# Split expert weights in device memory: one row of 24 KB per partition, or blocks of 128 rows of 4 KB

## What is computed

```python
mod = (silu(c) @ wmod).reshape(8, 6, 1, -1)
sa, ca, ga, sb, cb, gb = mod[:, 0], ..., mod[:, 5]
h = layernorm(x) * (1 + ca) + sa
x = x + ga * attn(h, ...)          # projections k, v, r; a decayed running sum of k*v; output projection
h = layernorm(x) * (1 + cb) + sb
x = x + gb * ffn(h, ...)

def moe_group(x2, router_w, wg, wu, wd, top_k):       # 32 experts, top_k = 2
    expert_weights, expert_indices = top_k(softmax(x2 @ router_w))
    # tokens sorted by expert, xs = x2[tok]
    gate, up = ragged_dot(xs, wg), ragged_dot(xs, wu)  # 512 -> 256
    ys = ragged_dot(silu(gate) * up, wd)               # 256 -> 512
    return zeros_like(x2).at[tok].add(ys * weight)

ffn = (moe_group(group 0) * 2 + moe_group(group 1) * 2) / 4
```

## Time and profile before

| | |
|---|---|
| median of 3 runs | 4911.22 us (4901.27 to 4916.95) |
| profiled execution, its own time | 4905.73 us |
| its span, first to last instruction | 4904.0 us |
| granted TensorE clock, mean | 0.971 |
| TensorE busy | 4580.8 us, 93% |
| DMA packets, bytes | 434624, 1152.46 MB, 235 GB/s |
| first stage, about | 0 to 1935 us |
| tile stage, about | 1935 to 4904 us |

### The profile page before, as it was taken

One profiled execution on the slowest core, in us unless ns is written; L12 is line 12 of the kernel. 1 busy time (PEld: TensorE's weight loads), 2 busy tenths in 40 slices (PEclk: granted clock), 3 DMA queues, 4 the chain that ended last, 5 costly groups with the idle time before them and its releaser, 6 DMA issues.

```text
span 4904.0 us, 89177 instructions
## 1 busy us (share of the span) xinstructions
PE 4580.8 (93%) x22649; PEld 3764.6 (77%) x22649; DVE 3080.2 (63%) x6077; ACT 1651.2 (34%) x4093; POOL 2858.1 (58%) x2300
## 2 busy tenths in 40 slices
PE   6999999999999995889999998999999999999998
PEld 4877777777777774667777777888788888888887
DVE  5999999999999996444444444444344444444443
ACT  2444444444444442222222222332222222222222
POOL 2577777777777776445444454555455555555554
PEclk8999999999999997899999999999999999999999
DMA  6767666666666674889899989998998988988887
GB/s 240 234 200 228 195 222 196 214 200 220 207 200 227 196 226 159 261 271 285 252 279 280 280 238 270 294 278 223 290 239 222 260 221 242 258 231 221 220 222 195
DMA packets 434624, 1152.46 MB, mean 235 GB/s; under 512 B 59361, under 2 KB 59362, under 8 KB 415666
## 3 DMA queue, kind: packets, MB, share of 16 engines
q0 software_dynamic: 182512, 454.27, 39.3%
q1 hardware_dynamic: 231106, 619.79, 36.6%
q10 hardware_dynamic: 20736, 75.51, 4.2%
HBM read 719.35 MB, written 463.57 MB: 241 GB/s over the span
## 4 chain that ended last, share of the span: by engine, by line
PE 42%; DMA 12%; issue 4%; POOL 2%; DVE 1%; POOLq 0%; SPq 0%; ACT 0%; DVEq 0%
PE ps L1316 12%; PE ps L1318 12%; PE ps L1317 12%; DMA out<-c_yo,c_idx 11%; PE ps L1325 4%; PE ps L1344 2%; POOL out L1307 1%; POOL c_xg L1274 1%; DMA c_wt<-wsp_d 0%; POOLq L1299 0%; DVE c_yo L1571 0%; POOL list_d L1279 0%; DMA list_d<-pairs,sidx 0%; DMA c_lists<-list_d,c_rowu 0%; DVE c_xl L1559 0%
## 5 line engine op out<-in xcount | busy, mean ns | idle before, releaser
L1307 POOL DMA_INDIRECT out<-c_yo,c_idx x576 | 915.1, 1589 | 933.9 <-DMA out<-c_yo,c_idx 512.5
L1316 PE MATMUL ps<-c_wt,c_xh 128*128 128x512 f32 x2304 | 964.1, 418 | 24.9 <-issue 16.8
L1318 PE MATMUL ps<-c_wt,c_xl 128*128 128x512 f32 x2304 | 910.3, 395 | 0.0
L1317 PE MATMUL ps<-c_wt,c_xh 128*128 128x512 f32 x2304 | 904.0, 392 | 0.0
L1274 POOL DMA_INDIRECT c_xg<-h2g_d,c_idx x576 | 565.0, 981 | 507.6 <-DVE c_yo L1571 400.5
L1555 DVE TENSOR_TENSOR c_hh<-ps,c_sil 128x256 f32<-128x256 f32 x576 | 244.2, 424 | 913.5 <-ACT c_sil L1398 843.5
L1571 DVE SCALAR_TENSOR_TENSOR c_yo<-ps,c_wc,c_xg 128x512 f32<-128x512 f32 x576 | 432.3, 750 | 529.2 <-PE ps L1318 261.5
L442 PE MATMUL ps<-xTh,wTh 128*128 128x512 f32 x1536 | 625.9, 407 | 53.5 <-DVE xTl L818 46.9
L1403 ACT CAST c_xh<-ps 128x512 fp32r<-128x512 f32 x576 | 339.2, 589 | 962.2 <-PE ps L1325 874.2
L709 POOL DMA_INDIRECT list_d<-pairs,sidx x496 | 545.5, 1100 | 188.5 <-issue 123.9
L1398 ACT ACTIVATE c_sil<-ps 128x256 f32<-128x256 f32 x576 | 221.3, 384 | 1177.1 <-PE ps L1318 1105.3
(11 more groups left out here) (199 smaller groups left out, 7776.2 us busy)
## 6 DMA issues: line engine op xcount, KB each, us to landing
c_wt<-wsp_d SPq DMA_DIRECT2D x69, 2048.0 KB
sraw<-wex SPq DMA_DIRECT2D x290, 256.0 KB
wsp_d<-shigh SPq DMA_DIRECT2D x288, 256.0 KB
wsp_d<-sraw SPq DMA_DIRECT2D x288, 256.0 KB
c_wt<-wsp_d SPq DMA_DIRECT2D x69, 1024.0 KB
xin<-x SPq DMA_DIRECT2D x34, 1024.0 KB
h2g_d<-mod_d SPq DMA_DIRECT2D x128, 256.0 KB
out<-xin SPq DMA_DIRECT2D x32, 1024.0 KB
```

The costliest lines, as they stand in the source:

```text
L1307: nc.gpsimd.indirect_dma_start(out=out, out_offset=bass.IndirectOffsetOnAxis(ap=idx[:, n:n + 1], axis=0), in_=yo[:, n % 4, :], in_offset=N ...
L1316: nc.tensor.matmul(o, lh, rh, start=first, stop=False)
L1317: nc.tensor.matmul(o, lh, rl, start=False, stop=False)
L1318: return nc.tensor.matmul(o, ll, rh, start=False, stop=last)
```

## The change

`wsp_d` gets another shape. Before it had 64 x 128 rows (expert, partition) of 6144 floats. Now it has for each expert 6 blocks (`NW`) of 128 rows of 1024 floats (`WCOL`): block k holds columns 1024 k to 1024 k + 1023 of what was the row. In memory, the rows of the 128 partitions of one block lie one behind the other, 4 KB each, and the next block of the same partition is 512 KB further on. The stores of SP and ACT write the same pieces to their new places. The load takes 4 blocks (gate and up) or 2 (down), so that each partition gets 4 or 2 rows of 4 KB in place of one of 16 or 8 KB. Nothing else changes: not the number of DMAs, nor their bytes, waits and order.

```diff
+WCOL = 1024
...
+    NW = 2 * WROW // WCOL
...
-    wsp_d = nc.dram_tensor("wsp_d", (GE * P, 2 * WROW), F32, kind="Internal").ap()
+    wsp_d = nc.dram_tensor("wsp_d", (GE * NW * P, WCOL), F32, kind="Internal").ap()
...
-                    return wex[0], bass.ds(b * (4 * P) + e * P, P), bass.ds(b * (4 * P) + e * P, P), part
-                return wex[1], bass.ds(b * (2 * P) + (e - 4) * P, P), bass.ds(b * (2 * P) + (E + e - 4) * P, P), part
+                    return wex[0], bass.ds(b * (4 * P) + e * P, P), b * 4 + e, part
+                return wex[1], bass.ds(b * (2 * P) + (e - 4) * P, P), b * 2 + (E + e - 4), part
...
-                    _, _, rows, part = split_at(b, j)
+                    _, _, ex, part = split_at(b, j)
                     for col, tile in zip(PARTS[part], (shigh[:, j % 2].bitcast(F32), sraw[:, j % 4])):
-                        sp.dma_start(wsp_d[rows, col:col + C], tile).then_inc(stg_out[j % 2], 16)
+                        rows = bass.ds(ex * (NW * P) + col // WCOL * P, P)
+                        sp.dma_start(wsp_d[rows, col % WCOL:col % WCOL + C], tile).then_inc(stg_out[j % 2], 16)
...
+            def load(u, e, a, z, sem_):
+                rows = bass.ds(e * (NW * P) + a // WCOL * P, (z - a) // WCOL * P)
+                sp.dma_start(wt[:, u, a:z].bitcast(F32).rearrange("p (n c) -> p n c", c=WCOL),
+                             wsp_d[rows, :].rearrange("(n p) c -> p n c", p=P)).then_inc(sem_, 16)
...
-                        sp.dma_start(wt[:, u, a:z].bitcast(F32), wsp_d[bass.ds(e * P, P), a:z]).then_inc(sem_, 16)
+                        load(u, e, a, z, sem_)
...
-                for col, tile in zip(((0, 2048), (1024, 3072), (4096, 5120))[k], (sgh[:, k].bitcast(F32), stg[:, k])):
-                    act.dma_start(wsp_d[rows, col:col + 1024], tile).then_inc(stg_out[k], 16)
+                for part, tile in zip(((0, 2), (1, 3), (4, 5))[k], (sgh[:, k].bitcast(F32), stg[:, k])):
+                    rows = bass.ds(x * (NW * P) + ((E + EA) * NW + part) * P, P)
+                    act.dma_start(wsp_d[rows, :], tile).then_inc(stg_out[k], 16)
```

More of the change, by code:

```diff
@@ L169, in stage_a @@
     xf, mod_d, h2g_d, list_d, wsp_d = L["xf"], L["mod_d"], L["h2g_d"], L["list_d"], L["wsp_d"]
-    ROWS = L["ROWS"]
+    ROWS, NW = L["ROWS"], L["NW"]
     R = TJ * G
@@ L1150, in stage_c @@
     GU = 2 * KC * 2 * H
+    NW = L["NW"]
     W = 4
@@ L1423, in split_out @@
             def split_out(x, k):
-                rows = bass.ds(x * P + (E + EA) * P, P)
                 act.wait_ge(stg_lo, job(x, k))
-                for col, tile in zip(((0, 2048), (1024, 3072), (4096, 5120))[k], (sgh[:, k].bitcast(F32), stg[:, k])):
-                    act.dma_start(wsp_d[rows, col:col + 1024], tile).then_inc(stg_out[k], 16)
+                for part, tile in zip(((0, 2), (1, 3), (4, 5))[k], (sgh[:, k].bitcast(F32), stg[:, k])):
+                    rows = bass.ds(x * (NW * P) + ((E + EA) * NW + part) * P, P)
+                    act.dma_start(wsp_d[rows, :], tile).then_inc(stg_out[k], 16)
             def turn(it, final=False, x=None, half=0):
```

## The result

The changed kernel takes 5003.7 us (median of 4 runs, 4995.98 to 5013.58), the kernel before beside it 4906.25 (4901.12 to 4916.95). The ratio is 1.0197, 95% interval 1.0167 to 1.0226, and the medians are 97 us apart. The profiled execution took 4997.59 us, 92 more than that of before.

What follows compares the result with a forecast made beforehand. TensorE was taken to bound the tile stage's second part, something else its first. Terms -45 + 62 + 25 + 8 = +50 on 4905.73 us gave 4956, or 4960 on the median's scale; range 4862 to 5035.

Steps and rivals of the forecast that it cites:

- The shape of the two parts: Tile stage: something other than TensorE paces 2070 to 3010 us, which gains; TensorE paces the later part, which loses.
- One row per turn: DMA engines: each queue gets one row per turn, whatever its size, from counts of 115, 124 and 120.
- Rival C: Weight loads: a partition's four pieces pass as one turn, so nothing changes; 4911 us, chance 0.09.
- q0 always has one waiting: Second part: q0 wants 16 rows per 4.8 us slot, but 16 turns take 5.4 us.
- Landing and its limit: Gate and up loads, second part: land 12.2 to 15.0 us after issue, against a limit of about 12.2.
- The single loads: Second part: 31 loads not close behind another, each late by 2.0 us; 62 us lost (0 to 87).
- the pairs: Second part: five loads issued under 10 us after another, 5 us lost at each; 25 us (10 to 45).
- The change of group: From 3463.66 us, five loads come right behind one another; one such wait, 8 us lost (0 to 15).
- The saving: First part: scatters held less by 21 loads; 23 to 103 us, middle 63, taken as 45.
- Scatters beside a load at 6 to 8 us: Expected sign in the changed profile: scatter-adds beside a weight load take 6 to 8 us.
- the 10.91 us: First part: scatter issued at 2387.57 beside weight loads, taken to fit 5.0 us of delay from 16 KB rows.
- Rival D: Weight loads: pieces 512 KB apart lower the rate; a tenth less gives 36 us more, 4996 us; chance 0.06.

Runs made afterwards that it cites:

- e1: Changed kernel with the gate and up load asked for earlier, once gate_up of the slot four before is done: 4900.05 us, ratio 0.9992.
- e8: Changed kernel with gathers from the ninth slot on fetching 16 rows instead of 128, computing something else: 4836.07 us, ratio 0.9857.
- e2: Kernel before, rows of 16 KB kept, with the gate and up load asked for earlier: 4901.13 us, ratio 0.9999.
- e6: Kernel before, store kept, loads cut into rows of 2 KB by gaps in the SBUF buffer: 5147.33 us, ratio 1.0500.
- e5: Changed kernel with early gate and up loads and two stores, 4 KB rows for the first group, as before for the second: 4875.12 us, ratio 0.9947.
- e3: Kernel before, store kept, loads cut into rows of 4 KB by gaps in the SBUF buffer: 5020.27 us, ratio 1.0241.
- e4: Changed kernel with blocks of 2048 columns instead of 1024, so rows of 8 KB: 4949.93 us, ratio 1.0098.
- e7: Kernel before, store kept, loads cut into rows of 8 KB by gaps in the SBUF buffer: 4928.14 us, ratio 1.0049.

## Why the prediction came out right, and where it did not

*The shape of the two parts, and the sign.* Right: the first part gained and the second lost, the second more. 5003.7 lies in the range; the point, 4960, was 44 low, most of it in the saving.

*One row per turn.* Right, though the counts over 5 us that I went by could not tell it from longer turns; the short stretches above do. The rule of 9 to 17 descriptors in a turn (the Trainium skill, DMA: Bandwidth & Descriptors, section Queues, rings and completion order) is not what these queues did, neither before nor after. Rival C is out. "q0 always has one waiting" was too much: in the 2 us up to 4062 q0 has 9 rows to 85 of the load's queue, and from 4059.5 to 4072.37, the load's whole time, 550 to 667.

*Landing and its limit.* Forecast 12.2 to 15.0 us, measured 14.4; limit 12.2. A load asked for earlier (e1) removes the loss; a load that q0 passes less often (e8) lands earlier.

*The size of the loss: partly luck.* The single loads and the pairs were put at 62 + 25 = 87 us, and those slots took 90.7 more. Only the first term was right. In the trace TensorE stands idle for 62 us in front of the `gate_up` of 30 single loads, 2.1 us each, and for 13 us at the second load of five pairs, 2.6 each where I had 5. The sum had no term for the clock: it took the matmuls to last as long as before, and they took 23 us longer. The clock goes with the waiting here: from slot 300 to 560 TensorE idled 0, 9, 55 and 89 us in e2, e1, the changed kernel and e6, and the granted clock was 1.00, 1.00, 0.99 and 0.96. The change of group was put at 8, measured 12.4.

*The saving, the term that was mis-sized.* -45 forecast, -11 measured in slots 25 to 189. It was made of two numbers, a relief of 63 us and 18 subtracted for loads that come late. The relief itself is 22 to 29 us: e1 and e5 against before and e2. That is at the lower end of my 23 to 103. Late loads take 11 to 15 of it away in the first part too (e1 takes 864.6 and e5 868.7, the changed kernel 879.8), a little less than the 18 that I had subtracted. So the error is the relief. VectorE's waits for a scatter-add from 2070 to 3010 us, before, then changed, then e1:

```profile
DVE c_yo L1571 <- DMA out<-c_yo,c_idx: 194.4, 62, 10.2
```

```profile
DVE c_yo L1580 <- DMA out<-c_yo,c_idx: 58.4, 23, 6.5
```

```profile
DVE c_yo L1582 <- DMA out<-c_yo,c_idx: 164.7, 55, 7.8
```

The fall from 194 to 58 us in the changed kernel looks like a great success, and it is mostly not one: TensorE came late with the results, so the buffers were free by then. With the loads in time 165 us of waiting are back. TensorE's own waits in the same 940 us say it more plainly, again before, changed, e1:

```profile
PE ps L1316 <- DVE c_hTl L1564: 63.9, 25, 8.0
```

```profile
PE ps L1325 <- issue: 33.7, 10, 10.9
PE ps L1325 <- DMA c_wt<-wsp_d: 17.7, 5, 5.0
PE ps L1325 <- DVE c_hTl L1573: 13.4, 6, 3.5
```

```profile
PE ps L1327 <- DVE c_hTl L1575: 48.6, 26, 5.5
```

The change took 50 us of waiting for `c_hTl` away and put most of it back in front of the weights (51 us in the first two rows; before, the same two had 13). Only 15 us of the waiting for `c_hTl` stay away once the loads are in time. "Scatters beside a load at 6 to 8 us" was wrong: in the chain of the changed kernel and in this stretch they still take up to 13.6 us (two more take 13.1 and 12.9),

```profile
2350.83 13.62 DMA out<-c_yo,c_idx
```

against 19 and 20 us for the longest before. So the 10.91 us on which I had built the price was not the typical case. What the longest ones wait for was not taken apart; a gather that stands in front of the scatter-add in q0, and ACT's rows, which take turns as well, are likely, and argued.

*The rest.* 7 us came from the two ends, which had no term. Of the waits I had named, "some 35 times and 60 to 100 us": the two rows of TensorE have 44 waits and 137 us, 28 waits and 105 us more than the same two before.

*Rival D* (place in memory): out by e3. If anything e3 is slower than the changed kernel, 1.0241 against 1.0197 with intervals that meet. In slots 189 to 283 and 300 to 560 the same matmuls took 1746 us in e3 and 1723 in the changed kernel, at a granted clock of 0.97 and 0.98 against 0.98 and 0.99. The pitch of 512 KB weighed there lies between the pieces of one partition; the partitions of a block lie 4 KB apart.

## What to carry to other kernels

Where DMA queues take turns row by row, as these did, the length of a row decides how the queues share the engines; how fast the engines are it changed by 1% (636 ns for four rows of 4 KB, 629 for one of 16). Shorter rows give time to the other queues and take it from this transfer; that pays only where the transfer has slack. So before cutting rows, compare its landing with the moment at which it is wanted, and get the slack first by asking for it earlier. A wait that shrinks after a change is no gain in itself: it may have moved behind a new wait further up. And price a wait of TensorE with the matmuls behind it: here 68 us of new idle time came with 23 us of slower matmuls.

## What was not expected

The landing of a 2 MB load among 16 rows per slot of other work went 10.8, 12.4, 14.4 to 14.9 and 17.1 us for rows of 16, 8, 4 and 2 KB: about 2 us for each halving, where the turns alone give 6.4, 7.8, 10.8 and 16.7. On top there are 4 to 5 us with long rows and next to nothing with the shortest, where q0 had a row for only every second turn (e6). A sum of turns is a good guide to the difference between two neighbours and a poor one over the whole range.

e4 and e7 have the same rows in their loads and differ in the place of the stores: rows of 2 KB that lie 8 KB apart in e4, 24 KB in e7. e4 is 22 us slower, and in its profile the first slot began at 2005 us, in e7's at 1986, while its tile stage is not the longer one. So the stores of the first stage may be the cause. Rows 4 KB apart (the changed kernel, first slot at 1986) show nothing of the kind. But this is one profile: in the ten others the first slot began between 1980 and 1993 us, the kernel before at the late end, so that 12 us are all that stands clear. Whether 8 KB is worse than 4 and 24, and why, was not tried, and stays open.
